# A four-layer graph network in five passes on one core: the last node groups of each pass, the stores of its last two tiles, and what the gathers of the max pass wait for

## The reference

```python
x = layernorm(x + L0(x))   # sum of neighbours, two 128x128 layers with relu, residual, layer norm with affine, relu
x = layernorm(x + L1(x))   # twice: l2-normalised rows summed over edges, scaled, @Wl + bl + h@Wr, l2-normalised; 128->256->128
x = layernorm(x + L2(x))   # max over edges of z[dst]@Wd + z[src]@Ws + w*ww + bm; then relu([z, agg]@W1 + b1)@W2 + b2
x = layernorm(x + L3(x))   # sum over edges of x[src]@W_type + b_type (two edge types), + x@W_self + b_self, relu
```

## Time and profile before

| | before |
|---|---|
| median of 3 runs | 3615.78 us (3613.31 to 3620.73) |
| profiled execution | 3613.41 us, its span 3608.6 us |
| granted TensorE clock, mean | 0.88 of full |
| PE busy | 2879.2 us (80%) |
| DVE busy | 1882.9 us (52%) |
| ACT busy | 960.5 us (27%) |
| POOL busy | 2376.1 us (66%) |

### The profile page before, as it was taken

The page is one execution under the profiler, slowest core; times in us unless marked ns, Lnnn a source line. Parts: engine busy times, 40 slices in busy tenths (PEclk is TensorE's granted clock), DMA queues, the critical chain, the costliest instruction groups (busy, mean ns, idle before and its releaser), DMA issues.

```text
span 3608.6 us, 57935 instructions
## 1 busy us (share of the span) xinstructions
PE 2879.2 (80%) x20827; PEld 2056.2 (57%) x20827; DVE 1882.9 (52%) x4798; ACT 960.5 (27%) x2506; POOL 2376.1 (66%) x2323
## 2 busy tenths in 40 slices
PE   3899986999989999999747676666766648888887
PEld 3455543666657888888635565555555534444444
DVE  7566665233332333333247888888888852323332
ACT  2566664223232333333211111111111210000000
POOL 4766662766636666666357777777777736777776
PEclk7899998999999999999856777787777868999999
DMA  6555444666647777777733333333333355656564
GB/s 168 183 179 182 169 171 146 222 225 212 214 168 241 256 263 263 252 264 256 234 86 79 84 87 85 84 87 85 86 85 84 94 199 190 212 193 210 196 200 128
DMA packets 277434, 615.38 MB, mean 171 GB/s; under 512 B 56962, under 2 KB 188506, under 8 KB 269724
## 3 DMA queue, kind: packets, MB, share of 16 engines
q1 hardware_dynamic: 172732, 367.98, 29.8%
q0 software_dynamic: 104416, 243.61, 24.1%
HBM read 470.79 MB, written 140.60 MB: 169 GB/s over the span
## 4 chain that ended last, share of the span: by engine, by line
PE 47%; DVE 13%; DMA 13%; POOL 10%; issue 9%; ACT 6%; SPq 1%; DVEq 1%; POOLq 0%; ACTq 0%
PE banks L1537 27%; DMA arena<-tab_l,ring_of_rows 7%; POOL ring_of_rows L1603 5%; DMA ring_of_rows<-message_pieces,span_sources 5%; PE banks L468 4%; POOL arena L430 4%; PE banks L1557 4%; PE banks L1555 3%; PE banks L380 3%; DVE arena L407 2%; DVE arena L1128 2%; PE banks L443 2%; PE banks L2221 1%; ACT junk L517 1%; PE banks L1652 1%
## 5 line engine op out<-in xcount | busy, mean ns | idle before, releaser
L1537 PE MATMUL banks<-arena 128*128 128x384 bf16 (+1 forms) x9212 | 1495.6, 312 | 26.0 <-DVE arena L1761 14.3
L1537 PEld LDWEIGHTS banks<-arena 128*128 128x128 bf16 x9212 | 882.6, 99 | 454.0 <-issue 49.3
L430 POOL DMA_INDIRECT arena<-tab_l,ring_of_rows x831 | 824.8, 993 | 322.6 <-issue 173.7
L380 PE MATMUL banks<-arena 128*128 x1758 | 458.4, 370 | 318.5 <-DVE arena L407 257.4
L1603 POOL DMA_INDIRECT arena<-h_pieces,span_sources x450 | 448.2, 996 | 276.7 <-PE banks L1557 132.1
L1603 POOL DMA_INDIRECT ring_of_rows<-message_pieces,span_sources x450 | 479.0, 1064 | 206.5 <-issue 110.9
L380 PEld LDWEIGHTS banks<-arena 128*128 128x128 f32 x1758 | 340.1, 251 | 424.0 <-issue 421.8
L1603 POOL DMA_INDIRECT ring_of_rows<-x_pieces,span_sources x270 | 307.7, 1140 | 181.1 <-PE banks L1555 109.8
L1555 PE MATMUL banks<-ring_of_rows,arena 128*128 128x384 bf16 x990 | 286.6, 336 | 142.5 <-DMA ring_of_rows<-message_pieces,span_sources 136.0
L1603 POOL DMA_INDIRECT ring_of_rows<-l_pieces,span_sources x270 | 268.7, 995 | 190.9 <-PE banks L1555 93.8
L1128 DVE SCALAR_TENSOR_TENSOR arena<-arena,ring_of_rows 128x128 f32<-128x128 f32 x831 | 285.0, 343 | 132.6 <-DMA arena<-tab_l,ring_of_rows 130.8
(11 more groups left out here) (241 smaller groups left out, 3113.5 us busy)
## 6 DMA issues: line engine op xcount, KB each, us to landing
arena<-edge_counts SPq DMA_DIRECT2D x82, 896.0 KB
arena<-edge_counts SPq DMA_DIRECT2D x82, 672.0 KB
edge_counts<-arena SPq DMA_DIRECT2D x34, 1568.0 KB
typed_counts<-arena SPq DMA_DIRECT2D x24, 1568.0 KB, 6.7
arena<-scan_mask SPq DMA_DIRECT2D x208, 128.0 KB, 3.2
arena<-typed_counts SPq DMA_DIRECT2D x24, 896.0 KB
arena<-typed_counts SPq DMA_DIRECT2D x24, 672.0 KB
arena<-tab_l,ring_of_rows POOLq DMA_INDIRECT x831, 3.1
```

The lines of the kernel that those rows point to most:

```text
L380: T.matmul(place(s, k.bank[:n_banks], cols), k.OH[:, s % OH_RING, :], k.RG[:, bass.ds(base, cols)], start=True, stop=True).then_inc(p.prod ...
L430: k.nc.gpsimd.indirect_dma_start(k.RG3[:, i % RING, at:at + width], None, table, bass.IndirectOffsetOnAxis(ap=k.SRC[:, i:i + 1], axis=0)). ...
L1537: t = T.matmul(k.bank[i % N_SUMS][:, 0:rows.shape[-1]], counts[:, s, :], rows, start=s == 0 and n == 0, stop=s == NT - 1 and n == len(term ...
```

## The change

1. `dense_schedule` places the stages of group 10 one position apart and those of group 11 inside what is left of the stream, so that no stage of group 11 is in `tail`.
2. The stores of groups 12 and 13 are issued by ACT, directly behind its own share of the `lo` or `table` stage, and no longer by SP.
3. Group 13 gets a slot of its own in `gbuf` (slot 3 of half 0, which group 12 of one tile leaves free), and its sum waits for group 10, no longer for group 11 (`buffer_before`). The weights of l2 that lay in that slot move.
4. In the SP stream of l1b, group 11's store stands in the main loop, and the `load`s of the linear part for groups 12 and 13 stand ahead of the `park` loads.
5. At the start of l2, POOL waits only for the stores of the table of groups 12 and 13 and for `park`.
6. At the end of l2, three of the four slab loads of l3 stand ahead of the last two loads of messages, and the fourth behind them.

```diff
@@ dense_schedule
     for g in range(NG - 2):
         first = max(max(done[j] for j in gtiles(g)) + 2, at + 1)
+        if g >= NG - 4:
+            room = min(room, len(stages) if g == NG - 4 else len(order) - first)
         for i, stage in enumerate(stages):
             at = first + i * room // len(stages)
@@
+def buffer_before(g):
+    return g - 3 if g == NG - 1 else g - 2
@@
-def store(k, p, what, g, dst, src):
+def store(k, p, what, g, dst, src, e=None):
+    e = e or k.nc.sync
     if g >= 2:
-        k.nc.sync.wait_ge(*p.stored(what, g - 2))
-    k.nc.sync.dma_start(dst, src).then_inc(p.stored(what, g)[0], 16)
+        e.wait_ge(*p.stored(what, g - 2))
+    e.dma_start(dst, src).then_inc(p.stored(what, g)[0], 16)
@@ gbuf
-    return k.GB[:, g % 2, 0:GROUPS[g], a:b]
+    n, t = (0, GMAX - 1) if g == NG - 1 else (g % 2, 0)
+    return k.GB[:, n, t:t + GROUPS[g], a:b]
@@ the sums of l1b on DVE (l0 and l1a alike, with lo and mid)
-            V.wait_ge(*p.stored("nodes", g - 2))
+            V.wait_ge(*p.stored("nodes", buffer_before(g)))
@@
+def store_nodes(k, p, g, e):
+    e.wait_ge(*p.at("table", g))
+    store(k, p, "l2", g, table_rows(k.tab["l2"], g), k.out3(g), e)
+    store(k, p, "nodes", g, k.nodes_dram[:, gslice(g), :], gbuf(k, g, 0, H2), e)
@@ dense_scalar_l1b, its tail (l0, l1a and l2 alike with "lo" and their own pieces)
     for stage, g in p.tail:
         node(stage, g)
+        if stage == "table":
+            store_nodes(k, p, g, A)
@@ the SP stream of l1b, behind its main loop
+    for stage, g in p.tail:
+        if stage == "load":
+            load(g)
     early = [g for stage, g in sum(p.due.values(), []) if stage == "table"]
@@
     for g in early:
         load_nodes(g)
-    for stage, g in p.tail:
-        if stage == "load":
-            load(g)
-        elif stage == "table":
-            table(g)
@@ the end of sync_l2
-        for i in range(2):
-            for h in range(2):
-                load_typed_slab(k, Plan(k, "l3", True), i, h)
+        for i, h in ((0, 0), (0, 1), (1, 0)):
+            load_typed_slab(k, Plan(k, "l3", True), i, h)
         for g in range(NG):
             if g not in early:
                 load_messages(k, p, g)
+        load_typed_slab(k, Plan(k, "l3", True), 1, 1)
@@ the start of a pass
+                    if layer == "l2" and regular and e is nc.gpsimd:
+                        for g in (NG - 2, NG - 1):
+                            e.wait_ge(*before.stored("l2", g))
+                        e.wait_ge(sem("park"), 16 * (3 + 2 + 2))
+                        write(k, plan)
+                        continue
```

More of the change, by code:

```diff
@@ L1007, in message_pieces, with store_messages @@
             (rows[:, :, H:H2], wide(region(k.ZT, g, 3 * H // 2).bitcast(BF16), 3 * H)))
+def store_messages(k, p, g, e):
+    e.wait_ge(*p.at("lo", g))
+    for n, (_, pieces) in enumerate(message_pieces(k, g)):
+        store(k, p, ("l3", "l3b")[n], g, k.pieces["l3"].rearrange("(t p k) c -> k p t c", p=P, k=2)[n][:, gslice(g), :], pieces, e)
 def tensor_l2(k, p):
@@ L1212, in scalar_l2 @@
         node(stage, g)
+        if stage == "lo":
+            store_messages(k, p, g, A)
 def gpsimd_l2(k, p):
@@ L1236, in node @@
             store(k, p, "l3", g, table_rows(k.tab["l3"], g, 2), wide(region(k.HT, g, H2), H2))
-        elif stage == "lo":
-            S.wait_ge(*p.at("lo", g))
-            for n, (_, pieces) in enumerate(message_pieces(k, g)):
-                store(k, p, ("l3", "l3b")[n], g, k.pieces["l3"].rearrange("(t p k) c -> k p t c", p=P, k=2)[n][:, gslice(g), :], pieces)
+        elif stage == "lo" and (stage, g) not in p.tail:
+            store_messages(k, p, g, S)
     def load_mask(c):
@@ L1623, in load_slab, with store_pieces @@
                             k.counts_dram[p.from_matrix[i]][:, a * P:b * P]).then_inc(slab_landed(k, p, i, h)[0], 16)
-def store_pieces(k, p, g, table, pieces, what):
-    k.nc.sync.wait_ge(*p.at("lo", g))
-    store(k, p, what, g, table_rows(table, g), pieces[:, gslice(g), :, :].rearrange("p t k c -> p t (k c)"))
+def store_pieces(k, p, g, table, pieces, what, e=None):
+    (e or k.nc.sync).wait_ge(*p.at("lo", g))
+    store(k, p, what, g, table_rows(table, g), pieces[:, gslice(g), :, :].rearrange("p t k c -> p t (k c)"), e)
 def row_pieces_hi(k, p, g, dst, src, stage):
@@ L1766, in sum_up @@
         if first_of_group(p, j) and g >= 2:
-            V.wait_ge(*p.at("lo", g - 2))
-            V.wait_ge(*p.at("mid", g - 2))
+            V.wait_ge(*p.at("lo", buffer_before(g)))
+            V.wait_ge(*p.at("mid", buffer_before(g)))
         V.tensor_reduce(row, sums_of(k, p, j), AX_X, ALU.add).then_inc(p.freed, 1)
@@ L1935, in dense_scalar_l0 @@
         node(stage, g)
+        if stage == "lo":
+            store_pieces(k, p, g, k.pieces["l1a"], k.XB, "pieces", A)
 def dense_gpsimd_l0(k, p):
@@ L1996, in dense_sync_l0 @@
             load_slab(k, Plan(k, "l1a", True), i, h)
-    for stage, g in p.tail:
-        if stage == "lo":
-            store_pieces(k, p, g, k.pieces["l1a"], k.XB, "pieces")
 def dense_tensor_l1a(k, p):
@@ L2164, in dense_scalar_l1a @@
         node(stage, g)
+        if stage == "lo":
+            store_pieces(k, p, g, k.pieces["l1b"], k.XP1, "pieces1", A)
 def dense_gpsimd_l1a(k, p):
@@ L2203, in dense_sync_l1a @@
     for stage, g in p.tail:
-        node(stage, g)
+        if stage != "lo":
+            node(stage, g)
 def tensor_typed_counts(k, i, u):
@@ L2411, in load @@
         S.dma_start(k.rows3(g), table_rows(k.aux1, g)).then_inc(k.sem(f"load_h1wr1_{g % 2}"), 16)
-    def table(g):
-        S.wait_ge(*p.at("table", g))
-        store(k, p, "l2", g, table_rows(k.tab["l2"], g), k.out3(g))
-        store(k, p, "nodes", g, k.nodes_dram[:, gslice(g), :], gbuf(k, g, 0, H2))
     def load_nodes(g):
@@ L2457, in dense_sync_l1b @@
             if stage == "table":
-                table(g)
+                store_nodes(k, p, g, S)
+    for stage, g in p.tail:
+        if stage == "load":
+            load(g)
     early = [g for stage, g in sum(p.due.values(), []) if stage == "table"]
@@ L3147, in build @@
         k.b1_2 = sb("l2_b1", [P, 1])
-        gap = [at(SRC_A + SRC_B + n * 4 * H2 + H2, 3 * H2) for n in range(2)]
-        k.w1_2, k.w2_2, k.b2_2, k.wst = wide(gap[0][:, 0:2 * H], H), gap[0][:, 2 * H:3 * H], gap[0][:, 3 * H:4 * H], gap[0][:, 4 * H:5 * H]
+        gap = [at(SRC_A + SRC_B + H2, 2 * H2), at(SRC_A + SRC_B + 4 * H2, 4 * H2)]
+        k.w1_2, k.w2_2, k.b2_2 = wide(gap[0][:, 0:2 * H], H), gap[0][:, 2 * H:3 * H], gap[0][:, 3 * H:4 * H]
         k.wdc, k.bdc, k.bs = wide(gap[1][:, 0:2 * H], H), gap[1][:, 2 * H:4 * H], gap[1][:, 4 * H:5 * H]
-        k.ww = gap[1][:, 5 * H:6 * H]
+        k.ww, k.wst = gap[1][:, 5 * H:6 * H], gap[1][:, 6 * H:7 * H]
         k.late_weights = (
```

## The result

| | before | changed |
|---|---|---|
| median of 4 runs | 3618.26 us (3613.31 to 3622.18) | 3562.18 us (3558.66 to 3569.46) |
| span of the profiled execution | 3608.6 us | 3557.2 us |
| ratio | | 0.9848, 95% interval 0.9827 to 0.9869 |

The kernel is 1.5% faster, 56 us by the medians; 38 were forecast. The median lies 16 us under the forecast of 3578 and 0.8 us under the low end of the range. The direction, the places and the mechanism at l2 were right; three terms were too small (l1b to l2, l1a to l1b, and l0 to l1a).

What follows compares the result with a forecast made beforehand. PE bounds passes until their last position, POOL's gathers bound l2, and a 52.1 us chain precedes l2. Gains 25.1 + 9 + 1.2 + 1.5 + 0.9 = 37.7 off 3613.4, plus 2.4 for the median: 3578 us, range 3563 to 3598.

Steps and rivals of the forecast that it cites:

- the mechanism at l2: Start of l2: earlier table stores and POOL's narrower wait let its gathers start at 1807.1 instead of 1833.2.
- l1b to l2: Turnover from l1b into l2: earlier table stores and first gathers bring the 17th gather forward, gaining 25.1 us.
- l1a to l1b: Turnover from l1a into l1b: `turn` comes 4 positions earlier, up to 3.7 us; 1.5 us taken.
- l0 to l1a: Turnover from l0 into l1a: group 11's `second` comes 3 positions earlier, up to 2.2 us; 1.2 us taken.
- The 52 us chain: End of l1b: stages of 11, SP's queue, 11's store, stages of 13, SP's queue, then l2; 52.1 us.
- Rival D: Ends of three passes: packed stages make PE wait, its clock drops to half, 8.6 us slower, 3624; chance 0.03.
- l2 to l3: Turnover from l2 into l3: last message stores land earlier, less 1 to 2 us for slower gathers; net 9 us.
- The 11.1 for the stores on ACT: End of l2: ACT issues within 0.9 us of the last piece, so the store lands at 2953.8, 11.1 us earlier.
- The landing, 5.6 us: End of l2: time for the last message store to land beside message loads, between about 3 and 7.2 us.
- the end of l3: End of l3: group 11 is finished within the stream, so a 0.93 us item goes; gain 0.9 us.
- A: Start of l2: DVE's start decides, gain 5.7 instead of 25.1 us, total 3597; chance 0.10.
- B: Start of l2: ACT's stores land late, behind SP's node loads; total 3590, or 3584 if half; chance 0.12.

## Why the prediction was right, and where it was short

*What bounds the kernel.* Right. The 52 us chain at l1b's end was what the edits cut, and l2, paced by its gathers (1.297 us each before, 1075.5 / 831 = 1.294 after), moved with its start.

*l1b to l2, 25.1.* It gave 28.7 + 1.3 = 30.0; the mechanism was right, three terms were off. (1) The landing of group 11's store was taken at 4.7 us, from a store that went out in full traffic. In the changed kernel it goes out ahead of the node loads and lands in 1778.31 - 1776.16 = 2.15. (2) The sum had 2.7 us for group 13's linear part to land behind that. The bias at 1781.14 waits 2.01 us for PE, as it did before, and for no load; (1) and (2) together are one gain, 1793.7 - (1781.14 + 9.6) = 3.0 us at the bias. (3) Gathers in full traffic were taken to be slower, 1 us over 16: they took 19.99 us at a DMA share of 1.04, against 20.46 before. The last stage of the chain was well sized: from the last table copy (1789.00) to the first gather 5.9 us, forecast 5.5. In the clock of the trace of before, with 9.6 us added, the first gather is at 1804.5 (forecast 1807.1), DVE's start at 1823.6 (1827), the 17th gather at 1824.5 (1828.9). The step of the prediction that both would come almost together holds: it had them 1.9 us apart, they were 1.0.

*Shares of the parts there.* They do not add. Undone alone, the narrow wait costs 18.2 us, ACT's stores 13.6, the schedule some 12.5 (on a slower chip), the slot's wait 2.5, together 46.8 where the boundary gained 32.1; done alone, the wait gains 9.7. Each part lets POOL use what the others free.

*l1a to l1b, 1.5.* It gave 7.5, and this was the step that failed most. The prediction halved the 3.6 of the positions and held the rest of the chain to be latency of small steps. Those steps are partly PE's own products at half clock. The changed kernel at the same place:

```profile
1059.87 1.60 PE L475 MATMUL banks<-l_wr,zt 128*128 128x128 f32 x12 [1.38 <-ACT zt L459]
...
1066.76 0.70 PE L475 MATMUL banks<-l_wl,zt 128*128 128x256 f32 x2
1067.29 0.59 PE L475 MATMUL banks<-l_wr,arena 128*128 128x256 f32 x2
...
1074.51 2.08 PE L475 MATMUL banks<-l_wr,zt 128*128 128x128 f32 x8 [3.04 <-ACT zt L459]
```

and its window of 23.5 us:

```profile
1051.03:1074.53 23.50, 12.22 (x73) 7.79 (x70) 10.68 (x42) 13.29 (x49) 0.00 (x0) 0.94 0.47 170
```

With products of the stream between the stages the granted clock is 0.94 in a window where it was 0.66. Group 11's `second` takes 1.60 instead of 2.93, and the eight of `first` of groups 12 and 13 end 1.98 us behind their start instead of 3.78 (1066.76 to 1068.74; 1074.43 to 1078.21): 3.1 of the 5.2 us by which `xturn` to the first gather got shorter. (5.2 is the most that any pair of profiles shows; with the 37.4 to 39.4 of the new schedule against 42.5 to 42.6 of the old it is 3.2 to 5.2.) The last `second` is at 2.08 again, since PE had waited before it. The other 2 us fit the positions, of which `hturn` shows 1.8 (13.73 us behind `xturn` before, 11.92 now). The 2.3 us that the pass gained ahead of `xturn` I can't assign: the kernel with the narrow wait alone, unchanged in l1a, differs from before by 2.1 us over that pass.

*Rival D, the clock.* It named the right cause with the wrong sign. I asked only whether the packed stages make PE wait in the stream; the clock stayed 1.00 there (22.60 us busy of 26.80 from 1035.80 to 1062.60, and 23.30 of 23.60 in l1b). I did not ask what the stream does for the stages. One of its readings was loose: the first stretch of the turnover, PE busy for 5.34 of 27.60 us, has a mean of 0.57, not 0.50.

*l2 to l3, 9.* It gave 8.7, by two misses that cancel. The 11.1 for the stores on ACT had no term for ACT's wait ahead of the first store: the prediction costed only the issue, with ACT "idle", but group 13's normalise stood behind, and its last piece was ready 2910.40 - 2870.46 = 39.9 us behind the last gather, where it was 2947.28 - 2910.05 = 37.2 before. That is 2.7 us more. ACT's wait explains 1.5 of them (addition to normalising, 1.65 before and 3.16 now); the other 1.2 lie ahead of the addition, 30.4 and 31.6 us behind the last gather, where the six profiles of the first chip range from 29.4 to 31.8, and I lay them to nothing. On the other side stood 2 us for slower gathers in full traffic; they were not slower (18 in 24.3 us both times, now at a DMA share of 1.04). The prediction's 1.43 us each came from two gathers of 2.30 and 1.90 us among the first seven of the trace of before. That the term came out is thus luck in part. The landing, 5.6 us, was right: the last store is issued by 2911.23, and DVE starts l3 at 2916.70.

*l0 to l1a, 1.2, and the end of l3, 0.9.* They gave 2.1 and 3.1. The first is real and was sized at half: from PE's last product with gathered rows to the first gather of l1a it is 26.9 to 27.0 us in the four profiles with the old schedule and 24.5 in the eight with the new one and nothing added, so 2.4. The prediction had up to 2.2 us there and took half, on the ground that the rest is latency and the two last tiles come behind it both ways; the whole of it came. The span from the first gather of l3 to the end is 640.9 and 642.9 us in the two profiles of the first chip with the old schedule and 639.8 to 642.5 in the four with the new, so the 3.1 may be as little as nothing.

*Rivals A and B.* A did not occur, but by a hair: DVE's start and the 16th gather lie within 1 us, and the kernel with the weights on ACT crossed the line. B is refuted by the stores that landed beside the node loads in 5.8 us. The weights on ACT's queue made SP's 24 loads end 7.5 us later, so the second queue added no bandwidth. What the second issuer saved was the time behind a sequencer held by long runs of loads, 13.6 and 8 us. The Trainium skill ("DMA: Bandwidth & Descriptors", section "Issuing engines are not separate DMA queues") says that DMAs started by any engine run on the same 16 DMA engines, and that a second issuer saves only sequencer time, usually small; the rows agree with the first, and at these two places the saving was not small.

## What to carry to other kernels

At a turnover between passes, look for the sequencer that issues a small store on which all wait, and what is queued in front of it; give that store to an engine whose own work it follows, and issue it behind that engine's last stage, since the wait for the data to be stored holds up everything behind it (1.5 us here). Put the last small stages between products of the long stream rather than behind it: besides the overlap, group 11's products ran at PE's full clock there (1.60 us instead of 2.93). And cost a landing from a store in the same traffic as the one to be moved.

## What the runs showed of the hardware

The mean granted clock was 0.66 over 23.5 us at l1a's end in which PE was busy for 9.8, and 1.00 when 72 products that nobody reads made it busy for 22.6 of them; two f32 products of 256 columns took 1.06 us in the one case and 0.59 in the other. Table stores of 192 and 64 KB landed in 2.2 and 2.3 us at DMA shares of 0.59 and 0.54; stores of the same sizes took 4.7 and 5.8 us at shares of 1.10 and 1.15. Gathers kept 1.25 us a piece at a share of 1.04. The chips differ by 14% on this kernel, nearly half of it in the pass of 831 gathers, 1077 against about 1295 us, where on a slower one POOL waits up to 5.6 us for a message.
